# Second attention pass of a graph network: broadcast keys, a bias row, sigmoid from PSUM, and the next layer's dot products at the end of a round

## The reference

```python
h = x @ W;  s = h @ a_src;  d = h @ a_dst
e = s[src] + d[dst];  e = where(e > 0, e, 0.2 * e)
w = exp(e - segment_max(e)[dst])
denom = segment_sum(w, dst)
out = segment_sum(w / (denom[dst] + 1e-16) * h[src], dst) + b
x = x + sigmoid(out)
```

## Time and profile before

| quantity | value |
|---|---|
| median of the runs | 13302.39 us |
| profiled execution, its own time | 13289.86 us |
| its span, first to last instruction | 13288.0 us |
| TensorE clock granted, mean | 0.728 |
| busy: PE, PE weight load, DVE, ACT, POOL | 51%, 38%, 38%, 30%, 50% |
| DMA | 171 GB/s mean |

### The profile page before, as it was taken

How to read it: one execution, slowest core, us unless ns; L and a number is a source line. 1 busy time by engine, 2 the same in 40 slices (tenths; PEclk the granted TensorE clock), 3 DMA queues, 4 the chain that set the end, 5 groups by cost and what they waited for, 6 DMA issues and landing times.

```text
span 13288.0 us, 166058 instructions
## 1 busy us (share of the span) xinstructions
PE 6817.6 (51%) x35028; PEld 5035.5 (38%) x35028; DVE 5103.2 (38%) x21345; ACT 3988.8 (30%) x8589; POOL 6591.9 (50%) x6351
## 2 busy tenths in 40 slices
PE   6777200077206730455322257776445888444888
PEld 3333100066105630455222235554224566323666
DVE  6777322366316641455322234443112333111444
ACT  7999200033002310233100024443112444111343
POOL 3444566544664566444677743334664333665000
PEclk9999655588657865677555578888556888555999
DMA  6777666644574457433233346655445777444998
GB/s 219 262 264 264 220 236 236 221 125 128 205 263 145 134 184 261 164 118 122 58 45 45 45 140 203 202 202 162 57 57 138 232 235 240 69 57 80 269 268 261
DMA packets 2128226, 2270.51 MB, mean 171 GB/s; under 512 B 234960, under 2 KB 1554869, under 8 KB 2121824
## 3 DMA queue, kind: packets, MB, share of 16 engines
q1 hardware_dynamic: 1798266, 1848.65, 42.0%
q0 software_dynamic: 321440, 418.37, 15.0%
q10 hardware_dynamic: 8390, 2.21, 0.1%
HBM read 1067.73 MB, written 1222.73 MB: 172 GB/s over the span
## 4 chain that ended last, share of the span: by engine, by line
DMA 15%; issue 10%; PE 9%; POOL 5%; another core or an unknown queue 4%; DVE 4%; SPq 3%; POOLq 1%; DVEq 0%; ACT 0%; ACTq 0%
DMA agg_d<-dO,fOI 11%; PE ps L1295 5%; DMA bXd<-agg_d 3%; POOL agg_d L801 3%; POOL bO L810 2%; PE ps L1272 2%; SPq L595 1%; PE ps L1282 1%; DVE aO L1805 1%; DVE bXd L1778 1%; PE ps L1270 1%; SPq L593 1%; DVE eE L1799 1%; SPq L602 0%
## 5 line engine op out<-in xcount | busy, mean ns | idle before, releaser
L862 POOL DMA_INDIRECT bXs<-x_d,fGI x784 | 798.0, 1018 | 1505.1 <-DMA x_d<-aH 1290.0
L801 POOL DMA_INDIRECT agg_d<-dO,fOI x784 | 1214.5, 1549 | 570.4 <-ACT dO L987 201.8
L1295 PE MATMUL ps<-W,aT 128*128 128x128 f32 x9408 | 1220.2, 293 | 23.5 <-ACT aS L1004 16.3
L1295 PEld LDWEIGHTS ps<-W,aT 128*128 128x128 f32 x9408 | 1194.9, 210 | 41.0 <-ACT aS L1004 27.1
L1282 PE MATMUL ps<-aS,W1X 128*128 128x512 f32 x2352 | 1206.8, 594 | 6.2 <-DMA eET<-eaT_d 6.0
L987 ACT COPY dO<-ps 128x128 f32<-128x128 f32 (+1 forms) x1176 | 318.1, 271 | 2795.7 <-DMA agg_d<-dO,fOI 1587.0
L1251 PE MATMUL ps<-bO,bNE 128*128 128x128 f32 x1568 | 568.3, 472 | 1082.8 <-ACT dO L987 1072.6
L1813 DVE TENSOR_TENSOR aH<-ps,B 128x512 f32<-128x512 f32 x588 | 406.5, 692 | 1861.5 <-PE ps L1295 1188.2
L1010 ACT ACTIVATE aT<-ps,BNT,BNS 128x512 f32<-128x512 f32 x1176 | 882.0, 774 | 616.2 <-PE ps L1283 576.4
L747 POOL DMA_INDIRECT bXs<-x_d,bGI x784 | 784.5, 1001 | 386.6 <-issue 246.2
L1738 DVE TENSOR_SCALAR bNE<-ps,dK 128x128 f32<-128x128 f32 x1176 | 317.6, 343 | 1558.0 <-PE ps L1229 1549.0
(11 more groups left out here) (260 smaller groups left out, 17857.3 us busy)
## 6 DMA issues: line engine op xcount, KB each, us to landing
agg_d<-zeros SPq DMA_DIRECT2D x788, 256.0 KB
bXd<-agg_d SPq DMA_DIRECT2D x784, 256.0 KB
agg_d<-zeros SPq DMA_DIRECT2D x394, 290.0 KB
bXd<-agg_d SPq DMA_DIRECT2D x392, 290.0 KB
x_d<-aO SPq DMA_DIRECT2D x392, 256.0 KB, 2.1
yg_d<-aYG SPq DMA_DIRECT2D x196, 512.0 KB, 3.1
aX<-yg_d SPq DMA_DIRECT2D x392, 256.0 KB, 4.4
x_d<-aH SPq DMA_DIRECT2D x392, 256.0 KB
```

Of the source, the lines that this page charges most:

```text
L801: pool.indirect_dma_start(agg_d[m][u % 2], bass.IndirectOffsetOnAxis(ap=index, axis=0), dO[:, u, 0:AW[m]], None, bounds_check=agg_last, oo ...
L862: pool.indirect_dma_start(fX[:, s, u, 0:C], None, gin_in[m], bass.IndirectOffsetOnAxis(ap=fGI[:, s, u:u + 1], axis=0), bounds_check=n_last ...
L1295: mm = pe.matmul(ps[6 + k][:, j * P:(j + 1) * P], eZ[:, k, h, j * P:(j + 1) * P], W2[:, m, h, :], start=(h == 0), stop=(h == 1))
```

## The change

Five edits of the second pass.

1. **Keys.** The keys are written once to HBM (`key_d`). SyncE loads each round's 1024 keys into all 128 partitions with one broadcast DMA (`pKB`), two rounds ahead. VectorE builds the masks from SBUF. `keys_along` on TensorE is gone.
2. **Bias row.** Row 32 of `pCW` holds the layer's bias, row 32 of the indicator tile `pIN` holds the denominators, loaded each round from a new `den_d`. The existing matmul (L1211) then adds denominator times bias, so that the scaling by the reciprocal gives the bias.
3. **Sigmoid from PSUM.** ScalarE computes `sigmoid(scale * psum)` in eight instructions of 128 elements straight from PSUM, between its copies and its diagonals. VectorE's eight L1680 are gone.
4. **PSUM.** The product of W alternates between ps4, ps5 and the freed ps0, ps1.
5. **Order on VectorE.** The sixteen dot products of round i-2 and their copy move from behind the masks to the end of the round, behind the final addition.

```diff
+        key_d = dram("key_d", (R, U * P))
+        den_d = dram("den_d", (R, U * P))
+        pKB = [aYG[:, 1 + k, :, :].rearrange("p j c -> p (j c)") for k in range(2)]
+        def rows_bank(s, u):
+            return ps[(4, 0)[s] + u // 4][:, (u % 4) * P:(u % 4 + 1) * P]
# SyncE
+            sp.dma_start(key_d.rearrange("r (h n) -> (r h) n", h=2), slT).then_inc(s_key, 16)
+                def load_keys(i, s):
+                    sp.dma_start(pKB[s], key_d[bass.ds(i, 1), :].to_broadcast([P, U * P])).then_inc(l_kb[s], 16)
                 def p2_round(i, rr, h, m=m):
+                    if inside(i + 2):
+                        sp.wait_ge(p_A, U * (r + 1))
+                        sp.sem_inc(s_gate, 1)
+                        load_keys(i + 2, s)
...
+                        sp.dma_start(pIN[32:33, s, :], den_d[bass.ds(i, 1), :]).then_inc(l_ix[s], 16)
...
+                sp.wait_ge(z_v, ZV * (m + 1))
+                sp.dma_start(den_d.rearrange("r (h n) -> (r h) n", h=2), slU).then_inc(s_den, 16)
                 load_rows_of(0, 0)
+                sp.wait_ge(z_p, ZP * (m + 1))
+                sp.wait_ge(s_key, 16)
+                for k in range(2):
+                    load_keys(k, k)
+                sp.wait_ge(s_den, 16 * (m + 1))
                 p_rounds(sp, p2_round)
# ScalarE, between the copies L969 and diagonals(i + 1)
+                    if inside(i - 1):
+                        act.wait_ge(p_fl, r)
+                        if past(i - 2):
+                            act.wait_ge(p_o, 2 * (r - 1))
+                        for u in range(U):
+                            if u % 4 == 0:
+                                act.wait_ge(p_rw, 2 * (r - 1) + u // 4 + 1)
+                            ins = act.activation(bTH[:, u, :], rows_bank(1 - s, u), ACT.Sigmoid,
+                                                 scale=pFL[:, 1 - s, 1, u:u + 1])
+                            if u % 4 == 3:
+                                ins.then_inc(p_sg, 1)
-                            act.wait_ge(p_z, 2 * (r - 1) + g + 1)
-                            act.activation(bTH[:, 4 * g:4 * g + 4, :], bTH[:, 4 * g:4 * g + 4, :], ACT.Sigmoid).then_inc(p_sg, 1)
+                act.copy(pCW[32:33, :], GB[32:33, m, :]).then_inc(p_cb, 1)
# TensorE
-                        if past(i - 2):
-                            pe.wait_ge(p_z, 2 * (r - 1))
+                        if past(i - 3):
+                            pe.wait_ge(p_sg, 2 * (r - 2))
...
-                    if inside(i + 2):
-                        pe.wait_ge(p_A, U * (r + 2))
-                        keys_along(i + 2, s)
# VectorE
-                        v.tensor_scalar(pA[s][:, u, :], ps[u // 4][:, (u % 4) * P:(u % 4 + 1) * P], pFE[:, s, 0, u:u + 1],
+                        v.tensor_scalar(pA[s][:, u, :], pKB[s][:, u * P:(u + 1) * P], pFE[:, s, 0, u:u + 1],
                                         pFE[:, s, 1, u:u + 1], ALU.is_equal, ALU.mult).then_inc(p_A, 1)
...
                     if inside(i - 1):
-                        for u in range(U):
-                            ...
-                            ins = v.scalar_tensor_tensor(out=bTH[:, u, :], in0=ps[4 + u // 4][:, ...],
-                                                         scalar=pFL[:, 1 - s, 1, u:u + 1], in1=GB[:, m, :], op0=ALU.mult,
-                                                         op1=ALU.add)
...
+                    if inside(i - 2) and m < M - 1:      # moved here, last in the round
+                        v.wait_ge(p_o, 2 * (r - 1))
...
+                p_rounds(v, p2_round)
+                v.wait_ge(s_den, 16 * (m + 1))
```

More of the change, by code:

```diff
@@ L1204, in p2_round @@
                         pe.wait_ge(p_ce, r)
[L1205 to L1207 removed]
+                        pe.wait_ge(l_ix[1 - s], 32 * (m * RS[1 - s] + h + (rr % 2 - 1) // 2 + 1))
+                        if past(i - 3):
+                            pe.wait_ge(p_sg, 2 * (r - 2))
                         for u in range(U):
[L1209 removed]
+                            pe.matmul(rows_bank(1 - s, u), pAT[1 - s][:, u * P:(u + 1) * P], W[:, m, :], start=True,
                                       stop=False)
[L1211 removed]
+                            mm = pe.matmul(rows_bank(1 - s, u), pIN[:, 1 - s, u * P:(u + 1) * P], pCW[:, :],
                                            start=False, stop=True)
@@ L1651, in p2_round @@
                     if inside(i + 1):
-                        masks(i + 1, 1 - s)
-                    if inside(i - 2) and m < M - 1:
-                        v.wait_ge(p_o, 2 * (r - 1))
-                        if m or past(i - 3):
-                            v.wait_ge(p_dc, r - 2)
-                        for u in range(U):
-                            v.tensor_tensor_reduce(bTL[:, u, :], bOs[s][:, u, 0:C], next_d, 1.0, 0.0, ALU.mult, ALU.add,
-                                                   bDT[:, 0, u:u + 1])
-                            ins = v.tensor_tensor_reduce(dO[:, u, 0:C], bOs[s][:, u, 0:C], next_s, 1.0, 0.0, ALU.mult, ALU.add,
-                                                         bDT[:, 1, u:u + 1])
-                        ins.then_inc(p_dt, 1)
-                        v.wait_ge(p_dt, r - 1)
-                        v.tensor_copy(SC[:, 1:3, bass.ds((i - 2) * U, U)], bDT[:, 0:2, :]).then_inc(p_dc, 1)
+                        masks(i + 1, 1 - s, h + s)
                     if inside(i):
                         if past(i - 2):
-                            v.wait_ge(p_z, 2 * (r - 1))
+                            v.wait_ge(p_sg, 2 * (r - 1))
                         v.tensor_copy(pFL[:, s, :, :], keys[:, 4:6, bass.ds(i * U, U)]).then_inc(p_fl, 1)
@@ L1675, in p2_round @@
                              ALU.add).then_inc(p_c, 1)
-                    if inside(i - 1):
-                        for u in range(U):
-                            if u % 4 == 0:
-                                v.wait_ge(p_rw, 2 * (r - 1) + u // 4 + 1)
-                            ins = v.scalar_tensor_tensor(out=bTH[:, u, :], in0=ps[4 + u // 4][:, (u % 4) * P:(u % 4 + 1) * P],
-                                                         scalar=pFL[:, 1 - s, 1, u:u + 1], in1=GB[:, m, :], op0=ALU.mult,
-                                                         op1=ALU.add)
-                            if u % 4 == 3:
-                                ins.then_inc(p_z, 1)
                     if inside(i - 1):
@@ L1711, in p2_round @@
                             v.tensor_scalar(bNG[:, :], bMV[:, :, 0], -1.0, None, ALU.mult).then_inc(p_mv, 1)
+                    if inside(i - 2) and m < M - 1:
+                        v.wait_ge(p_o, 2 * (r - 1))
+                        if m or past(i - 3):
+                            v.wait_ge(p_dc, r - 2)
+                        for u in range(U):
+                            v.tensor_tensor_reduce(bTL[:, u, :], bOs[s][:, u, 0:C], next_d, 1.0, 0.0, ALU.mult, ALU.add,
+                                                   bDT[:, 0, u:u + 1])
+                            ins = v.tensor_tensor_reduce(dO[:, u, 0:C], bOs[s][:, u, 0:C], next_s, 1.0, 0.0, ALU.mult, ALU.add,
+                                                         bDT[:, 1, u:u + 1])
+                        ins.then_inc(p_dt, 1)
+                        v.wait_ge(p_dt, r - 1)
+                        v.tensor_copy(SC[:, 1:3, bass.ds((i - 2) * U, U)], bDT[:, 0:2, :]).then_inc(p_dc, 1)
                 for k in range(2):
                     early_fields(k, k)
-                masks(0, 0)
+                masks(0, 0, 0)
                 p_rounds(v, p2_round)
+                v.wait_ge(s_den, 16 * (m + 1))
                 if m < M - 1:
```

32 lines of the change are left out of this document (12 added, 20 removed).

## The result

The changed kernel takes 13266.76 us (median of 9 runs, 13247.98 to 13280.84), the kernel before 13298.91 us beside it. The ratio is 0.9976, interval 0.9966 to 0.9985: 32 us less, where 109 were forecast. The profiled execution has a span of 13265.0 us (before 13288.0).

The account below looks back on a forecast made before the run. No engine is full in the second passes; a ring of waits bounds each round. Rounds -118 us and pass starts +9 give -109, 13181 us; with 12.5 us for the median of runs, 13193 us, range 12930 to 13440.

Parts of the forecast that it names:

- dot products last: VectorE in layers 0 and 1: dot products move ahead of the masks; scan and addition still wait for both, 0 us.
- start of a pass: Before a pass's first matmul: row load waits for reciprocals and stands with key loads; 3 us a layer, 9 us slower.
- What is late next: Layers 0 and 1: PE's undisturbed time sets POOL's gap at 4.2 us; round 15.3 to about 14.1, 118 us less.
- slow phase: Stretch of each round in layers 0 and 1 slowing several engines, from about 6 us after POOL's first scatter; cause unnamed.
- a coin toss: VectorE's scan, about 5.9 us after POOL's start, just where the slow phase begins; might move past it or not.
- The keys' term: Cheaper masks from SBUF take 0.95 us a round off DVE; PE loses 8 of 74 matmul instructions, 1.04 us.
- Row loads hidden: 3 us after: SyncE's row loads behind the keys still land before their matmuls; cover 5 us today, 3 after; uncovered, up to 2.3 us a round.
- the ring of waits: Layers 0 and 1: no engine full, waits close each round of about 15.3 us; 1.2 us less, 98 times.
- rival B: Slow phase takes back more: joined POOL batches catch PE mid-matmuls, a round costs 16.9 us, time 13458; chance 0.20.
- rival D: Masks from SBUF lock POOL out of writing scatter descriptors: up to 1.6 us a round, up to 13430; chance 0.07.
- A's end state: POOL never waits in layers 0 and 1: a round falls to 10.3 us, 500 us less, about 12810; chance 0.15.
- C: Gain hidden: PE's undisturbed time keeps the round at 15.3 us, with 9 us for the starts 13311; chance 0.13.

Follow-up runs that it names:

- e1: The changed kernel with only the move of the dot products taken back, behind the masks again; 0.9999 (0.999 to 1.0007) of the kernel before, on kind 2.

## Why the prediction was wrong

The sum on the chips of the result (kind 1), part by part:

| part | predicted, us | measured, us |
|---|---|---|
| sigmoid from PSUM, bias row | most of -118 | -55 (0.9959) |
| keys by DMA | the rest of it | +4 (1.0003) |
| dot products last | 0 | +24 (0.9977 against 0.9959) |
| start of a pass | +9 | inside the parts above; some +5 by the traces |
| all | -109 | -32, -35 |

-55 + 4 + 24 = -27, beside -32 and -35; each ratio carries some 15 us of interval. The second pair of banks wasn't tried alone; within these intervals nothing is left for it. The start of a pass is read from VectorE's first fields to the first marker: 13.3, 14.4 and 13.8 us before, 16.3, 15.0 and 15.2 after.

**The step that failed is "What is late next".** It let a round fall from 15.3 to 14.1 us because PE's undisturbed time would set POOL's gap to 4.2 us. (That gap and a batch of 10.3 make 14.5, which the section names as PE's; 14.1 is a middle between it and VectorE's 13.6. With 14.5 the sum would have been 78 us less instead of 118.) Measured over the batches of layer 1, POOL's gap has a median of 5.15 us before, 4.71 after, 4.60 with the sigmoid alone, 5.10 with the keys alone. The round became 14.85 (712.9 / 48), from 15.05. The timelines of the kernel with the sigmoid alone, DVE and then POOL, show why even the good part gives 0.3 us a round and not 1.8:

```profile
4411.51 0.08 DVE L1681 DVE_READ_ACCUMULATOR2_ANT bDT<- 128x1 f32 x1 [1.12 <-issue]
...
4412.20 0.17 DVE L1685 COPY SC<-bDT 128x16 f32 x1 [0.18 <-DVE bDT L1681]
...
4412.81 0.23 DVE L1487 TENSOR_TENSOR_SCAN pC<-pFL,pC,aYG 128x8 f32<-128x8 f32 x1
...
4413.42 0.69 DVE L1706 TENSOR_TENSOR bO<-bTH,bXd 128x512 f32<-128x512 f32 x1
4416.28 0.69 DVE L1706 TENSOR_TENSOR bO<-bTH,bXd 128x512 f32<-128x512 f32 x1 [2.17 <-ACT bTH L987]
```

```profile
4414.94 0.98 POOL L780 DMA_INDIRECT x_d<-bO,bOI  x1 [4.57 <-DVE bO L1706]
```

The slow phase catches whatever is under way. Without L1680 VectorE reaches the dot products earlier and is held in their last two, until 4411.51; the copy, the fields, the scan and the addition still follow: 3.4 us from 4411.5 to 4414.94. PE is held in the second half of its rows in the same way. I had counted 2 us there, with dot products, sigmoids and PE's rows all done before the phase began.

The step also took PE's need of undisturbed time as given, 9.9 us at the clock it had, less the transposes. In layer 1's pass the keys alone do leave it less (busy 472 us at a clock of 0.80, before 529 at 0.84), and the sigmoid alone doesn't (539 at 0.84); the change has the fewer instructions and is busy 526 us at 0.77. What this costs the ring of kind 1 wasn't isolated.

**"Dot products last: 0" was wrong by 24 us**, and the prediction had named a reason it could be, the scan at 5.9 us after POOL's start as "a coin toss". The coin isn't what costs: in layer 1 the scan comes when POOL's batch is over (10.1 us behind its first scatter, or later) in 41 of 44 rounds of the kernel after, and in 43 of 44 with the sigmoid alone, where the dot products haven't moved. What the move adds behind the slow phase is the masks (2.14 us, in the timeline above); beside them run ScalarE's copy and sigmoids, which the addition needs too, so that less than 2.14 us of it shows. On kind 2 the same move costs 0.26% without the sigmoid edit, 0.2% or less beside it (e1 0.9999 and the change 1.0008, on two chips).

**The keys' term was mis-sized twice.** On VectorE it is 0.45 us a round, since I took the mean latency (403 and 284 ns) for what an instruction adds. And little of it reaches the ring: with the keys alone the passes of layers 0 and 1 take 744.6 and 716.8 us, 13 less than before, layer 2's 959.9, 6 more (inside the bounds given), and the runs say +4. "Row loads hidden: 3 us after" held on kind 1, whose rounds are 15 us; on kind 2, with rounds of 10.5 us, that cover is gone and the keys cost 83 us.

**What the prediction didn't see** is more than half of what layers 0 and 1 gained: a stop of VectorE at the loop's branch in layer 0. Layer 0's pass fell 35 us, layer 1's 10. `p_rounds` makes 11 bodies of four rounds, so its branch is taken ten times. In layer 0 of the kernel before, VectorE's next instruction comes 6.9 to 8.3 us after each of the ten, and 0.5 us after the eleventh, which falls through; in layer 1 it comes 0.6 us after each. Kernel before on kind 2, DVE:

```profile
2750.32 1.41 DVE L1694 TENSOR_TENSOR aT<-bTH,bXd 128x512 f32<-128x512 f32 x2
2758.20 0.18 DVE L1634 COPY pFE<-keys 128x24 f32 x1 [6.48 <-issue]
```

The waits of the pass of layer 0, one fence a kernel: before; after; the sigmoid alone; the keys alone (all kind 1; us in total, times, longest).

```profile
DVE pFE L1634 <- issue: 55.8, 8, 7.7
DVE pFE L1634 <- ACT bSW L954: 15.7, 3, 6.8
```

```profile
DVE pFE L1659 <- issue: 5.7, 11, 0.6
```

```profile
DVE pFE L1655 <- issue: 7.0, 4, 1.8
```

```profile
DVE pFE L1639 <- issue: 40.9, 6, 7.2
```

The profile puts two of the ten stops of the kernel before, and four of the ten with the keys alone, to ScalarE's diagonals instead of "issue"; they stand behind the branch like the others. Together the ten are 69 us, and layer 0's pass was 29.6 us longer than layer 1's. Without them it is 4.4 us longer in the kernel after and 3.0 with the sigmoid alone. So of the change's 35 us in layer 0 some 25 are the stop, and the ring of waits that I had priced gave about 10 us a layer, 0.2 us a round instead of 1.2. On kind 2 the sigmoid alone takes layer 0 from 565.0 to 509.7 us and layer 1 from 503.0 to 501.4: there the stop is nearly all of its gain.

The stop goes in every kernel without L1680, 8 instructions a round off VectorE, on both kinds of chip, and in none that keeps it, wherever keys and dot products stand. With the dot products moved alone it is even longer (8.3 to 9.2 us against 6.1 to 6.7, both kind 2), which is most of what that move costs there. The prediction took one average round for both layers and priced a stop at the branch at nothing; the joined batches of the earlier trace rows, from which it priced rival B, stand right behind such a stop (VectorE idle 7.69 us, to 2881.47).

The page Runtime: NRT & Kernel Launch ("Instruction fetch mechanics") of the Trainium skill says that a taken branch can force a fetch of its target before execution goes on. The stops, at taken branches and not at the one that falls through, agree; the prediction cited the rule, weighed it only against the slow phase and dropped it. Why layer 0 alone, and why 8 instructions fewer end it, wasn't isolated; the length of the body alone isn't it, since the trace shows 277 instructions of VectorE from branch to branch in layer 0, with the stop, and 287 in layer 1, without.

Right were: the rival D has no support (masks at 0.274 us; the 70 scatters of layer 1 that have masks beside them still take 0.98 us, the median), DMA share 0.53 to 0.55 for 0.50, layer 2 within 10 us, the batch of POOL unchanged. Rivals: A's end state, POOL never waiting, is what layer 1 shows on kind 2, before the change too. B didn't come on kind 1. C, the gain hidden, was the nearest description for the keys.

**Open:** what the slow phase is. It goes with the chip and not with the program: the same kernel before has it in one trace and not in the other, and the two kinds differ by some 930 us. Layer 2's pass is the same on both (953.8 and 953.6 us); the passes of layers 0 and 1, and the time between passes (656 and 657 against 592 and 599 us), are not. The transposes aren't its cause (the keys alone, on chip 10, have rounds of 15 us without them), nor are full DMA engines (above). Nor does it begin at a fixed place in POOL's batch, as the prediction had it: in the round of the kernel after shown above VectorE's last dot products show the first such waits 4.6 us behind POOL's first scatter and TensorE's rows 8.8 us behind it. While it lasts, an engine that is held starts one instruction in about 0.7 or 1.4 us, on waits named "issue" (TensorE at 4407.22, 4407.94, 4408.68, 4410.09 and 4411.51 with the sigmoid alone). That would fit instructions that reach the engines late. It is a rival as untested as the scatters themselves: no kernel without them was run, and none made to test this.

## What to carry to other kernels

Work taken off an engine is worth what the ring behind the last wait loses, so ask for each edit where the moved instruction stands when the next disturbance begins; an order that puts needed work (masks, scan) behind unneeded work (dot products) pays for it. A new load belongs behind the loads that someone waits for: on kind 2 the same 512 KB a round cost 0.67% in front and 0.02%, nothing within the interval, behind. Time each part alone before keeping a bundle: here one part gave it all, and the others took half of it back on kind 1 and all of it on kind 2. And look at each loop's branch by itself before averaging over rounds: ten stops of 7 us gave 25 us here, beside 20 from the ring that I had worked out.

## What the runs showed that I had not expected

The same program ran at 12352 to 12397 us on three chips and at 13299 to 13318 us on two (and on that of the result), and a part's worth depended on which: the keys 1.0067 against 1.0003, while the sigmoid gave 0.9961 and 0.9959. A taken branch can cost an engine 7 us in one loop and 0.6 us in a longer one of the same form. An instruction's mean ns (364) and what it adds to its engine (274) differ where they overlap; only the second belongs in a sum.
